# Second attention's score operands in a row-interleaved layout, staged from SBUF for the first group of heads; two stages' weights loaded one stage earlier

## What is computed

```python
x = x + attn_a(_layernorm(x), ...)   # index scores choose keys; 16 heads, low-rank keys and values, rope
x = x + ffn(_layernorm(x), ...)      # 8 experts, 2 chosen, plus a shared one
x = x + attn_b(_layernorm(x), ...)
x = x + ffn(_layernorm(x), ...)

def attn_b(h, w_dkv, w_q, w_uk, w_uv, w_o):
    c_kv = h @ w_dkv.T                                   # 2048 x 128
    q = (h @ w_q.T).reshape(B, S, 16, 16)
    k = (c_kv @ w_uk.T).reshape(B, S, 16, 16)
    v = (c_kv @ w_uv.T).reshape(B, S, 16, 16)
    scores = q @ k.T * 16 ** -0.5 - 0.0625 * (i - j)     # j <= i only
    return (softmax(scores) @ v) @ w_o.T
```

## Time and profile before

| what | us |
|---|---|
| median of 3 executions (2766.78 to 2771.85) | 2769.87 |
| the profiled execution, its own time | 2778.29 |
| its span, first to last instruction | 2776.4 |
| PE busy / DVE / ACT / POOL | 2332.4 / 1789.3 / 1678.2 / 709.6 |
| mean granted TensorE clock | 0.908 |

### The profile page before, as it was taken

The page is one execution under the profiler, slowest core; times in us unless marked ns, Lnnn a source line. Parts: engine busy times, 40 slices in busy tenths (PEclk is TensorE's granted clock), DMA queues, the critical chain, the costliest instruction groups (busy, mean ns, idle before and its releaser), DMA issues. The chain is left out here.

```text
span 2776.4 us, 42489 instructions
## 1 busy us (share of the span) xinstructions
PE 2332.4 (84%) x12560; PEld 1566.9 (56%) x12561; DVE 1789.3 (64%) x3726; ACT 1678.2 (60%) x3051; POOL 709.6 (26%) x974
## 2 busy tenths in 40 slices
PE   5956694668999999999999997984559999997985
PEld 2533362347777778787878784653234444424653
DVE  4788798865777677677767775424167877814523
ACT  2679587946777777687777774232217777753232
POOL 0214412433222422242234311352100000000253
PEclk9978897889999999999999998997759999967998
DMA  1011101141000100000000004123640303000124
GB/s 48 0 38 61 61 0 49 57 139 47 16 17 9 31 14 12 14 28 16 13 20 20 5 1 123 43 76 94 175 61 2 47 9 40 1 1 25 42 76 134
DMA packets 78250, 115.62 MB, mean 42 GB/s; under 512 B 24658, under 2 KB 52146, under 8 KB 75058
## 3 DMA queue, kind: packets, MB, share of 16 engines
q1 hardware_dynamic: 67796, 91.62, 12.1%
q0 software_dynamic: 10240, 21.38, 2.6%
HBM read 70.63 MB, written 41.94 MB: 41 GB/s over the span
## 5 line engine op out<-in xcount | busy, mean ns | idle before, releaser
L1394 DVE TENSOR_TENSOR aa_pt_lo<-psum,aa_pt_hi 128x512 fp32r<-128x512 f32 x544 | 350.4, 685 | 82.6 <-ACT aa_pt_hi L1324 79.8
L1845 DVE TENSOR_REDUCE ab_part_max<-psum 128x2 f32<-128x1024 f32 (+3 forms) x320 | 327.2, 1062 | 116.8 <-PE psum L1683 114.9
L1787 ACT ACTIVATE ab_prob<-psum 128x512 f32<-128x512 f32 (+3 forms) x640 | 297.9, 542 | 121.3 <-PE psum L1712 117.3
L1324 ACT ACTIVATE aa_pt_hi<-psum 128x512 fp32r<-128x512 f32 x544 | 297.3, 598 | 116.4 <-PE psum L1254 113.5
L1381 DVE CUSTOM_DVE_ANT_0 aa_prob<-psum,bias 128x512 f32<-128x512 f32 (+2 forms) x480 | 278.6, 598 | 114.4 <-PE psum L1244 95.8
L1208 POOL TENSOR_TENSOR x<-aa_y_out,x 128x256 f32<-128x256 f32 x256 | 188.3, 735 | 355.1 <-ACT aa_y_out L1342 310.3
L1242 PE MATMUL psum<-ka_hi,aa_q_hi 128*128 128x512 f32 (+3 forms) x640 | 267.8, 418 | 10.9 <-POOL aa_q_lo L1176 8.1
L1254 PE MATMUL psum<-ident,aa_prob 128*128 128x128 f32 x1600 | 252.9, 274 | 6.8 <-issue 5.5
L1316 ACT ACTIVATE aa_prob<-aa_prob,aa_neg_max 128x128 f32<-128x128 f32 (+11 forms) x192 | 227.9, 1188 | 44.1 <-DVE aa_neg_max L1387 42.3
L1712 PE MATMUL psum<-ab_q_stack,ab_k_stack 50*128 50x512 f32 (+3 forms) x640 | 242.6, 458 | 13.6 <-ACT ab_prob L1787 9.2
L1265 PE MATMUL psum<-aa_pt_hi,c_stack 128*128 128x512 f32 x544 | 233.2, 429 | 5.9 <-ACT aa_out_t L1331 4.3
(11 more groups left out here) (338 smaller groups left out, 4859.4 us busy)
## 6 DMA issues: line engine op xcount, KB each, us to landing
q_rows<-ixt_q_out SPq DMA_DIRECT2D x64, 256.0 KB, 2.1
aa_q_row<-q_rows SPq DMA_DIRECT2D x64, 256.0 KB, 2.6
f_back<-done SPq DMA_DIRECT2D x16, 512.0 KB, 7.4
w<-in_w SPq DMA_DIRECT2D x6, 896.0 KB, 11.3
x<-in_hidden SPq DMA_DIRECT2D x2, 2048.0 KB, 11.4
ab_q_stack<-stash_q_hi SPq DMA_DIRECT2D x32, 128.0 KB, 10.8
ab_k_stack<-stash_k_hi SPq DMA_DIRECT2D x32, 128.0 KB, 12.1
ixt_wq_n<-in_Wq_nope_T SPq DMA_DIRECT2D x2, 1024.0 KB, 6.2
```

The source lines that it names most:

```text
L1324: nc.scalar.activation(pt_hi[(TB[t] + j) % RING][:], turn_bank[(TB[t] + j) % RING], ACT.Copy).then_inc(pt_hi_done, 1)
L1394: nc.vector.tensor_tensor(pt_lo[ring][:], turn_bank[(TB[t] + j) % RING], pt_hi[ring][:].bitcast(F32), ALU.subtract).then_inc(pt_lo_done, 1)
L1787: nc.scalar.activation(prob[i % 2][h][:, 0:w], t_bank[slot % RING][:, 0:w], ACT.Exp).then_inc(t_taken, 1)
L1845: nc.vector.tensor_reduce(part_max[e % 2][:, at:at + 5:4, part], s_pair[pair % 2][:, :, 0:w], AX.X, ALU.max).then_inc(s_used, 1)
```

## The change

**The index stage.** ln1 is now called inside `index_mask`, with the 15 loads of "ixp" as its `load`.

**`prepare_a`.** w_dkv, norm_w, cos, sin and both copies of w_uv get a place above all that `index_threshold` uses and are issued by SP in the second `index_threshold`, behind that one's own loads. `prepare_a` itself loads only Wo and x. PE makes five of the eight head pairs, then transposes the keys, then makes the other three; the mean goes to bank 0.

**`prepare_b`.** The four weights are loaded beside ln3. The parts come in the order q0, k0, q1, k1. There is no room of their own for all high and low parts now: three tiles `own`, the four stacks of set 1, and xT's second half (for the last low part). Group 0's heads are rows 0 to 63 of part 0, and SP copies them straight from there into the stacks of set 0, 12 DMAs of 32 partitions. The stash gets the other 64 rows of the 0 parts and all of the 1 parts. The block's end waits for the 12 copies and for the four stash writes of the 0 parts; those of the 1 parts go on. Stacks of set 0 are zeroed here (q by DVE, k by POOL), and POOL writes their constant rows (16 DMAs of one row); the masks `after` and `halves` are made here too.

**`attention_b`.** A stack's rows are interleaved: rows 0, 4, 8, ... hold the first, 1, 5, 9, ... the second and 2, 6, 10, ... the third of the three row sets, for both heads of a stack in one DMA of 32 rows with a partition step of 4. Row 3 is the position bias, row 63 the maximum, the others of every fourth row are zero. The score matmuls take 63 and 64 rows instead of 49 and 50. Before it stages group 1, SP waits for the last stash write, loads the constant rows, and waits for POOL, which has waited for all stash writes and zeroed the four stacks of set 1; then POOL issues 16 DMAs of constant rows, waits for them, and only then begins with event 0.

The diff, cut to its core:

```diff
-R_LO, R_HI2, R_ALIBI, R_MAX = 16, 32, 48, 49
+R_ALIBI, R_MAX = 3, 63
+SAME_ROWS = 2 * 2 * 2 * 2
+STAGE = 2 * 2 * 3
...
+            layernorm(nc, "ln1", x, xT, bank, const["ident"], mean, rstd, load=load)
...
                     sp.dma_start(rope[:, n], arg[name]).then_inc(rope_in, 16)
+                if load_early is not None:
+                    load_early(sp)
...
-                for n in range(HA // 2):
+                for n in range(EARLY_HEADS):
+                    absorb(n)
                 pe.wait_ge(keys_ready, 1)
...
+                for n in range(EARLY_HEADS, HA // 2):
+                    absorb(n)
+                pe.wait_ge(lo_done, 1)
...
+        own = [sb(f"own{p}", [P, S], F32R) for p in range(3)]
+        later = q_stack[1] + k_stack[1]
+        hi = [own[0], own[2], later[1], later[3]]
+        lo = [own[1], later[0], later[2], None]
+        lo[3] = xT[:, 1, :].bitcast(F32R)
...
+                sp.wait_ge(zeroed[0], 4)
+                for j, (name, m) in enumerate(JOBS[0:2]):
+                    sp.wait_ge(lo_done, NCH * (j + 1))
+                    stage_stacks(sp, (q_stack if name == "q" else k_stack)[0], name,
+                                 lambda part, n: (hi, lo)[part == "lo"][j][n * 2 * DHB:(n + 1) * 2 * DHB, :].bitcast(F32),
+                                 staged[0])
+                for j, (name, m) in enumerate(JOBS):
+                    sp.wait_ge(lo_done, NCH * (j + 1))
+                    rows = slice(0, P) if m else slice(GB * DHB, P)
+                    for part, have in (("hi", hi), ("lo", lo)):
+                        sp.dma_start(stash[f"{name}_{part}"][m * P + rows.start:(m + 1) * P, :],
+                                     have[j][rows, :].bitcast(F32)).then_inc(stashed[j], 16)
+                sp.wait_ge(staged[0], STAGE * 16)
+                for early in range(2):
+                    sp.wait_ge(stashed[early], 2 * 16)
...
+def stage_stacks(sp, stacks, name, source, staged):
+    for n, stack in enumerate(stacks):
+        for place, part in enumerate(("hi", "lo", "hi") if name == "q" else ("hi", "hi", "lo")):
+            sp.dma_start(stack[place:P:4, :].bitcast(F32), source(part, n)).then_inc(staged, 16)
...
             @block.sync
             def _(sp):
+                sp.wait_ge(stashed[3], 2 * 16)
                 sp.dma_start(same[0:2, :, :], arg["b_same"]).then_inc(same_loaded, 16)
...
+                sp.wait_ge(zeroed[1], 4)
+                stage_group(sp, 1, stash, q_stack[1], k_stack[1], staged[1])
...
             @block.gpsimd
             def _(pool):
                 pool.wait_ge(same_loaded, 16)
+                for job in range(4):
+                    pool.wait_ge(stashed[job], 2 * 16)
+                for stack in q_stack[1] + k_stack[1]:
+                    nc.gpsimd.memset(stack[:].bitcast(F32), 0.0).then_inc(zeroed[1], 1)
+                pool.wait_ge(zeroed[1], 4)
+                same_rows(nc, same, q_stack[1], k_stack[1], same_in[1])
+                pool.wait_ge(same_in[1], SAME_ROWS * 16)
                 for e in range(EVENTS):
```

More of the change, by code:

```diff
@@ L219, in _, with index_mask @@
                     turn_verdict(NCH - 1)
[L222 removed]
+def index_mask(nc, arg, x, xT, psum, bank, const, mean, rstd, bias, bias_at, q_rows, load_early):
     with Phase(nc, "ix") as phase:
@@ L970, in _, with keep @@
                 nc.scalar.activation(rms[:], ss[:], ACT.Sqrt).then_inc(rms_ready, 1)
-                for n in range(HA // 2):
+                def keep(n):
                     act.wait_ge(absorbed, n + 1)
@@ L974, in _ @@
                                          ACT.Copy).then_inc(absorbed_stored, 1)
-                act.wait_ge(keys_ready, 1)
-                nc.scalar.activation(c_stack[:, :, 0:RANK], keys[:, :, 0:RANK], ACT.Copy).then_inc(c_done, 1)
+                for n in range(EARLY_HEADS):
+                    keep(n)
                 for n in range(4):
@@ L1421, in _, with prepare_b @@
                 walk(dve, before, run, dve_order)
-def prepare_b(nc, arg, xT, bank, stash, values):
+def prepare_b(nc, arg, xT, bank, weights, loaded, stash, q_stack, k_stack, zeroed, staged, stashed, same_in, after, halves, values):
     with Phase(nc, "pb") as phase:
         sb, sem = phase.sb, phase.sem
-        w_dkv = sb("w_dkv", [P, KC, KVB])
-        w_q = sb("w_q", [P, KC, D])
-        w_uk = sb("w_uk", [P, D])
-        w_uv = sb("w_uv", [P, D])
+        w_dkv, w_q, w_uk, w_uv = weights
+        JOBS = [("q", 0), ("k", 0), ("q", 1), ("k", 1)]
         c_kv = sb("c_kv", [P, S])
-        part = {name: sb(name, [P, KC, S], F32R) for name in ("q_hi", "q_lo", "k_hi", "k_lo")}
-        loaded = sem("loaded")
+        own = [sb(f"own{p}", [P, S], F32R) for p in range(3)]
[3 more added lines that the diff above has]
+        lo[3] = xT[:, 1, :].bitcast(F32R)
+        after_wide = sb("after_wide", [P, 2, 2, P])
+        halves_wide = sb("halves_wide", [P, 2, P])
+        same = values[:].rearrange("p h t d -> p (h t d)")[:, 0:2 * S].rearrange("p (w n) -> p w n", w=2)
+        same_loaded = sem("same_loaded")
+        consts_in = sem("consts_in")
+        ones_done = sem("ones_done")
         done = sem("done")
@@ L1459, in _ @@
             @block.gpsimd
             def _(pool):
+                for stack in k_stack[0]:
+                    nc.gpsimd.memset(stack[:].bitcast(F32), 0.0).then_inc(zeroed[0], 1)
+                pool.wait_ge(same_loaded, 16)
+                pool.wait_ge(zeroed[0], 4)
+                same_rows(nc, same, q_stack[0], k_stack[0], same_in)
+                pool.wait_ge(same_in, SAME_ROWS * 16)
                 nc.gpsimd.memset(values[:, :, :, DHB:], 1.0).then_inc(ones_done, 1)
@@ L1511, in _ @@
             def _(dve):
-                for n in range(FIRST_Q, FIRST_V):
-                    m, c = divmod((n - FIRST_Q) % (KC * NCH), NCH)
-                    name, scale = ("q", SCALE_B) if n < FIRST_K else ("k", 1.0)
+                for stack in q_stack[0]:
+                    nc.vector.memset(stack[:].bitcast(F32), 0.0).then_inc(zeroed[0], 1)
+                nc.vector.memset(bank[7], 0.0)
+                dve.wait_ge(consts_in, 2 * 16)
+                nc.vector.tensor_copy(after[:], after_wide[:])
@@ L1519, in _, with stage_group @@
                                                    op0=ALU.mult, op1=ALU.subtract).then_inc(lo_done, 1)
-def attention_b(nc, arg, x, xT, psum, bank, const, stash, values):
-    GB = 4
+def stage_stacks(sp, stacks, name, source, staged):
+    for n, stack in enumerate(stacks):
+        for place, part in enumerate(("hi", "lo", "hi") if name == "q" else ("hi", "hi", "lo")):
+            sp.dma_start(stack[place:P:4, :].bitcast(F32), source(part, n)).then_inc(staged, 16)
+def stage_group(sp, g, stash, q_stack, k_stack, staged):
+    for name, stacks in (("q", q_stack), ("k", k_stack)):
+        stage_stacks(sp, stacks, name,
+                     lambda part, n: stash[f"{name}_{part}"][(g * GB + 2 * n) * DHB:(g * GB + 2 * n + 2) * DHB, :], staged)
@@ new lines, in same_rows, with attention_b @@
+def same_rows(nc, same, q_stack, k_stack, same_in):
+    for n in range(2):
+        for half in range(2):
+            for which, stack in enumerate((q_stack, k_stack)):
+                for row, at in enumerate((R_ALIBI, R_MAX)):
+                    nc.gpsimd.dma_start(stack[n][half * 64 + at:half * 64 + at + 1, :].bitcast(F32),
+                                        same[row:row + 1, which, :]).then_inc(same_in, 16)
+def attention_b(nc, arg, x, xT, psum, bank, const, stash, q_stack, k_stack, zeroed, staged, stashed, same_in, after, halves, values):
@@ L2360, in _ @@
                 nc.vector.tensor_copy(const["causal"][:], causal_wide[:])
-        layernorm(nc, "ln1", x, xT, bank, const["ident"], mean, rstd)
         with ExitStack() as a:
```

222 lines of the change are left out of this document (106 added, 116 removed).

## The result

| | before | changed |
|---|---|---|
| median of 4 executions each | 2770.37 us (2766.78 to 2771.85) | 2696.86 us (2694.78 to 2699.81) |
| the profiled execution | 2778.29 us | 2696.14 us |
| its span and mean granted clock | 2776.4 us, 0.908 | 2694.1 us, 0.928 |

The ratio is 0.9737, 95% interval [0.972, 0.9754]. The gain is 73.5 us between the medians and 82.2 between the profiled executions, where the forecast had 56.0.

What follows compares the result with a forecast made beforehand. PE was taken to bound the attentions' long stretches, leaving gains only in its waits: 12.4 + 2.7 + 41.9 - 1.0 (an added phase boundary) = 56.0 us, giving a median of 2713.9 us, range 2702 to 2736.

Steps and rivals of the forecast that it cites:

- What bounds the kernel: PE limits both attentions' long stretches; gains lie in its waits at index weights, `prepare_a` and the second attention's start.
- Index weights, 12.4: Index projection: loads issued beside ln1 let PE start at 25.7 instead of 38.12, gaining 12.4 us, range 10 to 14.
- `prepare_a`, 2.7: Early w_dkv and Wo and five pairs first gain 2.7 us; 0 if PE restarts at low clock, 5 if products run faster.
- The second attention's start, 42.0: Early weights and direct copies at 209 GB/s let PE start at 1990.3 instead of 2032.29, 42.0 us gained.
- its better case: Rival, chance 0.10: direct copies at 359 GB/s, 63.2 us gained in all, 2706.7; some 3 less if PE keeps its clock.
- What is late next: Transposed scores, second attention: POOL's chain to event 0 and PE's lead end together at 2027.7; 41.9 us gained.
- Slow copies: Rival, chance 0.15: group 0's direct copies run at the old 122 GB/s; 38.2 us gained in all, 2731.7.
- overtaking: Rival, chance 0.05: late stash writes of the 1 parts share the DMA engines, block end 11.7 us later, 2725.6.
- POOL as the wait: Rival, chance 0.14 (8 us or more): POOL's memsets and landings delay event 0, chain 18.7 us later, 2732.6.
- Slower by contraction rows: Rival, chance 0.02: score matmul time follows contraction rows, 63 and 64 for 49 and 50, adding 133.6 us, 2847.5.
- list of what would show it wrong: PE waits over 8 us for event 0, `staged` wait ends after 2000, or long-stretch clock below 0.96.
- The base: Profiled execution before, 2778.3, stands 8.4 us above the median 2769.87, so the forecast 2722.3 becomes 2713.9 for the median.

Runs made afterwards that it cites:

- run with late writes: Changed kernel with the four 1 MB stash writes of the 1 parts issued at attention_b's start and only set 1's k stacks zeroed: 2697.66 us.
- zero rows by memset: Kernel before with second-attention scores over 63 and 64 rows, 14 of them zero, zeros from memsets on DVE and POOL: 2758.05 us, ratio 0.9934.
- the run again beside it: The changed kernel, unedited, run once more for a second profile: 2697.28 us, ratio 0.9726.

## Why the prediction was right or wrong

- **What bounds the kernel, right as far as it went.** The three waits named are where 55 of the 82 us came from (11.9, 1.4 and 42.1).
- **Index weights, 12.4.** The start came 11.7 us earlier (38.12 to 26.40; 25.7 was forecast), and 11.85 were left at `prepare_a`. Undone alone it is 10.7 us by the marks; by the medians it is 14.6 across batches, and 8 to 11 against the kernel before beside each. By the marks the term stands within its "10 to 14".
- **`prepare_a`, 2.7.** 1.35 in the first pair of profiles, 0.8 in the second. The forecast named the case: "0 if PE restarts at the low clock after its wait". PE did restart so, and the wait for the keys was 4.54 us. The term failed on the choice between the two ends. With all eight pairs ahead, 39.35 us, the block would have given 6.3.
- **The second attention's start, 42.0: measured 42.1, in part by luck.** Two misses cancelled. The copies began 15.4 us after PE's first product and not 18.1, since that product took 7.10 us for 9.86 (the clock, which the forecast had only as "some 3 less" in its better case). From there to PE's start it took 31.3 us and not 28.5: the copies ran at 185 GB/s, not 209. The Trainium skill (SBUF — State Buffer, section on the DMA port swizzle) gives 196 and 189 GB/s for partitions 0 to 63 and 0 to 31. By that rule, the trace agrees within 6%. In the second pair of profiles the gain was 46.0.
- **What is late next, right in its order.** A POOL memset was 1.78 us against 1.7, event 0 was issued at 2006.4, 30.5 us after PE's first score against "some 34", and PE's lead took 37.4 us against 37.3. The chain has 3.7 us to spare where the forecast had none: the stash had landed 7.8 us after PE's start, not 10.2, and POOL began 2.5 us behind it, not 3.3.
- **Slow copies, overtaking, POOL as the wait.** None came in full. Of overtaking, the run with late writes shows about 2 us.
- **Slower by contraction rows.** Refuted: 468 and 434 ns at 63 and 64 rows against 473 and 458, and no difference at the same clock (two in 0.79 and 0.80 us).
- **The step that failed** is the one ahead of the sum: "The change leaves the number and order of these matmuls alone, so what can be won lies where PE stands still". The window of the earlier trace rows ends at 2400 and has a mean granted clock of 0.96. The 64 us from 2449 on, at 0.53, were not read, and the mean hid the start. What the runs showed in its place: with the number and order of these matmuls unchanged, and PE busy 94% of the time before, the last stretch fell from 65.98 to 48.07 us since the clock rose, and zero rows alone brought 44.65. The page of the kernel before had the sign, in 40 slices of 69.4 us, shares in tenths. The 36th slice, from 2429 to 2499 us, has a 9 for PE and a 6 for its clock:

```profile
PE   5956694668999999999999997984559999997985
PEclk9978897889999999999999998997759999967998
```

This row, of the kernel before, is of the 63 us behind the first transposed score; its clock, 0.86, stands for 0.50 at first and 1.00 later:

```profile
2070.00:2133.00 63.00, 61.58 (x501) 31.85 (x500) 48.41 (x48) 43.60 (x94) 1.99 (x4) 0.86 0.01 1
```

Before, the clock came back to 1.00 some 17 us behind the first transposed score; in the changed kernel and with zero rows by memset it took 7 to 8 us.

The forecast's list of what would show it wrong looks for the opposite sign alone: "a granted clock in the long stretch below 0.96 (rows of a matmul cost more than time)". Rows gained time: 24.8 us here, 27.4 between the profiles of before and before with zero rows, 19.2 between the second profiles of before and changed.
- **The base.** The forecast took the profiled execution's 8.4 us above its median as a constant. Beside other runs the kernel before had medians of 2774 to 2777 us, so the base was no outlier, and 73.5 us is the low side of the gain: by the run again beside it, 2773.9 to 2697.3, it is 76.6.

## What to carry to other kernels

Look for stretches where PE is over 90% busy and the granted clock is near 0.5. There a matmul's busy time is long because the clock is low, and a wait table shows nothing, since nobody waits. In this kernel a layout that fills more contraction rows, even with zeros, brought the clock back for the price of a memset; elsewhere it has to be tried. After an edit that moves work past a wait, check the wait's length and the rows behind it: with waits of 2.0 and 3.4 to 3.6 us the matmuls of `prepare_a` kept full clock, with 4.2 to 4.8 they did not. The length of the last wait is no sure sign: behind 1.7 us the first product of `prepare_b` took 7.1 us in most profiles and 8.8 in three. A single profile of each kernel can therefore be off by some us in a short stretch; compare two. A staging copy wants many partitions; whether it goes straight or by DRAM counted for little here.

## What the runs showed of the hardware

- With fourteen zero rows more in every score matmul, the last stretch of the kernel before went from 65.98 and 65.97 us (two profiles of 49 and 50 rows, granted clock 0.53 and 0.52) to 44.65 us in both of its profiles with 63 and 64 rows (granted clock 1.00). The kernel got 17 us faster by computing with zeros. Why the clock follows the rows, no run here shows, and one unprofiled execution of the kernel before, 2749.99 us at a mean clock of 0.922, suggests that 49 and 50 rows do not always lose it.
- At the low clock PE was 94% busy in that stretch, and its clock still did not rise. Of the twelve profiles with 64 rows seven took 44.7 us for it and five took 46.2 to 51.0, the latter with a short stay at the low clock (0.52 over 10 us in the changed kernel).
- The 256 KB copies over 32 partitions ran at 185 GB/s from SBUF to SBUF with the DMA engines 92% busy (186 GB/s at 99% in the 6 us from 1950), and at 292 GB/s from DRAM with them 80% busy. The first window's last 5 us also hold the first stash writes.
- On SP, issuing such a copy took 1.1 us from SBUF (six in 6.55; the later ones up to 2.5) and 0.6 out of DRAM. The stash writes issued behind the copies took up to 2.4 us each, where such a write took 0.33 in the earlier trace rows; so the price is at least in part that of a DMA queue that is full, and no run parts this from the source of the copy.
